# Row scatters of a routed-experts kernel: spaced over attention's units, the last 24 at the start of the last stage

## The reference

```python
logits = xt @ router_w.T + routing_bias
probs = jax.nn.sigmoid(logits)
topk_p, topk_idx = jax.lax.top_k(probs, TOP_K)          # TOP_K = 2
topk_p = topk_p / jnp.sum(topk_p, axis=-1, keepdims=True)
...
h = jax.nn.silu(g) * u                                  # per expert
y = jnp.einsum('tei,ehi->teh', h, wd)
routed = jnp.einsum('te,teh->th', w, y)
return (shared + routed).reshape(orig_shape)
```

## Time and profile before

| what | value |
|---|---|
| median of 3 runs | 1726.43 us (1722.62 to 1728.62) |
| the profiled execution | 1709.23 us |
| its span | 1707.4 us |
| mean granted TensorE clock | 0.945 |
| attention, first to last instruction | 595.45 to 1159.44 us |
| last stage begins | 1165.07 us |

### The profile page before, as it was taken

One profiled execution on the slowest core, in us unless ns is written; L12 is line 12 of the kernel. 1 busy time (PEld: TensorE's weight loads), 2 busy tenths in 40 slices (PEclk: granted clock), 3 DMA queues, 4 the chain that ended last, 5 costly groups with the idle time before them and its releaser, 6 DMA issues. The chain is left out here.

```text
span 1707.4 us, 28845 instructions
## 1 busy us (share of the span) xinstructions
PE 1508.1 (88%) x10278; PEld 1160.2 (68%) x10278; DVE 1105.0 (65%) x2324; ACT 903.8 (53%) x1123; POOL 448.2 (26%) x439
## 2 busy tenths in 40 slices
PE   5899999698999888999988987765899999999996
PEld 4788888577878652444343433344689999999985
DVE  5577776678878845546735645243457778777757
ACT  2566546255555435565554554532246777777741
POOL 1122232130101122211423333145202333333324
PEclk8999999889999979999988999976799999999998
DMA  7000000210000002100000000014116888888844
GB/s 260 1 1 0 0 0 0 75 40 1 0 0 0 7 19 89 64 1 1 21 7 27 1 26 27 10 48 166 46 37 189 230 237 234 231 235 236 227 116 148
DMA packets 65068, 130.47 MB, mean 76 GB/s; under 512 B 8377, under 2 KB 38882, under 8 KB 64482
## 3 DMA queue, kind: packets, MB, share of 16 engines
q1 hardware_dynamic: 49922, 108.14, 20.6%
q0 software_dynamic: 15072, 21.37, 5.7%
HBM read 97.50 MB, written 32.00 MB: 76 GB/s over the span
## 5 line engine op out<-in xcount | busy, mean ns | idle before, releaser
L1745 ACT ACTIVATE at_wide<-at_sc_ps 128x2048 f32<-128x2048 f32 x128 | 240.6, 1880 | 176.6 <-PE at_sc_ps L1590 169.7
L1590 PE MATMUL at_sc_ps<-at_qT,at_kT 32*128 32x512 f32 x1024 | 152.4, 665 | 59.7 <-ACT at_wide L1745 55.1
L2168 POOL DMA_INDIRECT sums<-e_y,e_row_ids x78 | 121.7, 1560 | 313.8 <-ACT e_y L2323 301.9
L52 PE MATMUL e_gate_ps<-e_h_parts,e_w 128*128 128x256 f32 (+1 forms) x1128 | 179.3, 307 | 10.4 <-DVE e_w L2374 3.9
L52 PE MATMUL e_up_ps<-e_h_parts,e_w 128*128 128x256 f32 (+1 forms) x1128 | 175.8, 303 | 0.0
L2374 DVE TENSOR_TENSOR e_w<-e_raw,e_w 128x1024 fp32r<-128x1024 f32 x123 | 147.3, 1223 | 42.0 <-ACT e_w L2276 42.0
L52 PEld LDWEIGHTS e_gate_ps<-e_h_parts,e_w 128*128 128x128 f32 x1128 | 156.8, 195 | 18.8 <-issue 7.0
L52 PEld LDWEIGHTS e_up_ps<-e_h_parts,e_w 128*128 128x128 f32 x1128 | 156.1, 193 | 8.3
L1604 PE MATMUL at_o_ps<-at_wide,at_v_ones 128*32 128x512 f32 x1024 | 142.4, 629 | 1.1 <-ACT at_wide L1745 1.1
L2239 PE MATMUL e_down_ps<-e_w,e_hidden 128*128 128x256 f32 x936 | 127.9, 286 | 1.1 <-DVE e_hidden L2423 1.1
L2276 ACT ACTIVATE e_w<-e_raw 128x1024 fp32r<-128x1024 f32 x123 | 125.3, 1048 | 4.0 <-DMA e_raw<-in_experts 4.0
(11 more groups left out here) (348 smaller groups left out, 2718.2 us busy)
## 6 DMA issues: line engine op xcount, KB each, us to landing
e_raw<-in_experts SPq DMA_DIRECT2D x123, 512.0 KB
e_rows_in<-slots SPq DMA_DIRECT2D x39, 272.0 KB
sums<-shared SPq DMA_DIRECT2D x17, 256.0 KB
x<-in_L_attn_x SPq DMA_DIRECT2D x8, 512.0 KB, 9.5
gate<-gates SPq DMA_DIRECT2D x4, 1024.0 KB, 4.7
out<-x SPq DMA_DIRECT2D x7, 512.0 KB, 3.1
e_sums<-sums SPq DMA_DIRECT2D x4, 512.0 KB, 4.6
shared<-sums SPq DMA_DIRECT2D x4, 512.0 KB, 5.2
```

The lines of the kernel that those rows point to most:

```text
L52: last = pe.matmul(out, left(i), right(j), start=n == 0, stop=n == len(steps) - 1)
L1590: last = nc.tensor.matmul(sc_ps[:, m, :], kT[strip, par, quad % 2, quad // 2, k * P:(k + 1) * P], qT[strip, par, quad // 2, :], start=True ...
L1745: nc.scalar.activation(wide[:, u % 2, :], sc_ps[:].rearrange("p n s -> p (n s)"), ACT.Sigmoid, scale=float(HD) ** -0.5).then_inc(sig_done, 1)
L2168: pool.indirect_dma_start(c.sums_dram[:, :], bass.IndirectOffsetOnAxis(ap=row_ids[:, j % 2, t:t + 1], axis=0), y[:, j % 2, t, :], None, co ...
```

## The change

In attention, `scatter` is split into `tag` (waits and tag copies) and single scatters. In iteration b of 3 and more the tags of batch b - 3 and its first scatter come right behind `place_values`; the others follow one by one between GpSimd's other pieces, each waiting until 3, 5, 7, ... 15 sigmoids of the iteration are done. The scatters of batches 5, 6 and 7 leave attention and the place behind it: GpSimd issues all 24 as the last stage begins. (A pace by `hidden_split` is written for those from number `UNPACED` = 24 on, which are none.) The rows of batch 7 are made and kept in the last stage, behind its first step, which is written out ahead of the loop for this. The padding is one plain DMA per expert on SP's queue, with its address read from `pads`.

```diff
-                    if b >= 3:
-                        ds.scatter(pool, b - 3)
...
+                def scatter(b, n, unit=None):
+
+                    if b >= 3:
+                        if unit is not None:
+                            pool.wait_ge(sig_done, UNITS * b + unit)
+                        ds.scatter(pool, b - 3, n)
...
                     if coming:
                         place_values(b + 1, 1 - par, early)
+                    if b >= 3:
+                        ds.tag(pool, b - 3)
+                    scatter(b, 0)
+                    if coming:
                         times_cos(b + 1, 0)
+                    scatter(b, 1, 3)
+                    if coming:
                         times_cos(b + 1, 1)
+                    scatter(b, 2, 5)
                     if past:
                         bias_x(b - 1)
+                    scatter(b, 3, 7)
+                    if past:
                         norm.invert(pool, b - 1)
+                    scatter(b, 4, 9)
                     if coming:
                         times_cos(b + 1, 2)
+                    scatter(b, 5, 11)
+                    if coming:
                         times_cos(b + 1, 3)
+                    scatter(b, 6, 13)
+                    scatter(b, 7, 15)
...
                 bias_x(B - 1)
-                ds.scatter(pool, B - 3)
                 norm.invert(pool, B - 1)
-                ds.scatter(pool, B - 2)
...
-                pe.wait_ge(ds.rows_kept, 2 * (B - 1))
-                ds.make_rows(pe, B - 1, 0, sc_ps[:, 0, :])
-                ds.make_rows(pe, B - 1, 1, sc_ps[:, 1, :])
...
-                ds.keep_rows(act, B - 1, 0, sc_ps[:, 0, :])
-                ds.keep_rows(act, B - 1, 1, sc_ps[:, 1, :])
...
+                for e in range(E):
+                    at = sp.value_load(pads[0:1, e:e + 1], min_val=0, max_val=E * REGION - TS)
+                    sp.dma_start(c.slots_dram[bass.ds(at, TS)].rearrange("(p t) r -> p t r", p=P), ds.empty
+                                 ).then_inc(ds.padded, 16)
...
-                ds.scatter(pool, B - 1)
-                pool.wait_ge(listed, 1)
-                for e in range(E):
-                    for t in range(TT):
-                        pool.indirect_dma_start(c.slots_dram, bass.IndirectOffsetOnAxis(ap=pads[:, e, t:t + 1], axis=0),
-                                                ds.empty[:, t, :], None).then_inc(ds.padded, 16)
+                LATE = 3
+                for k in range(LATE * 2 * NT):
+                    b = B - LATE + k // (2 * NT)
+                    if k % (2 * NT) == 0:
+                        ds.tag(pool, b)
+                    if k >= UNPACED:
+                        pool.wait_ge(hidden_split, k - UNPACED + 1)
+                    ds.scatter(pool, b, k % (2 * NT))
...
-                with pe.Fori(0, BEFORE) as n:
+                step(0, 0, 1)
+                pe.wait_ge(ds.placed, B)
+                pe.wait_ge(listed, 1)
+                for half in range(2):
+                    ds.make_rows(pe, B - 1, half, tp_ps[:, half, :])
+                with pe.Fori(1, BEFORE) as n:
                     step(n, n * IC, 1)
+                pe.wait_ge(ds.rows_kept, 2 * B)
...
-                with act.Fori(0, BEFORE - 1) as n:
+                step(0, 0, 1)
+                for half in range(2):
+                    ds.keep_rows(act, B - 1, half, tp_ps[:, half, :])
+                with act.Fori(1, BEFORE - 1) as n:
                     step(n, n * IC, n + 1)
...
-                    nc.vector.scalar_tensor_tensor(out=pads[:], in0=ends[:].unsqueeze(2).broadcast_to([P, E, TT]), scalar=BIG,
-                                                   in1=pad_at[:].unsqueeze(1).broadcast_to([P, E, TT]), op0=ALU.add, op1=ALU.add)
+                    nc.vector.tensor_scalar(pads[:], ends[:], BIG, None, ALU.add)
```

More of the change, by code:

```diff
@@ L1346, in keep_rows, with tag @@
                                   ACT.Copy).then_inc(self.rows_kept, 1)
-    def scatter(self, pool, b):
+    def tag(self, pool, b):
         c = self.c
@@ L1358, in scatter @@
         pool.wait_ge(self.placed, b + 1)
[L1359 to L1363, removed]
+    def scatter(self, pool, b, n):
+        t, which = n // 2, n % 2
+        at = NT * b + t
+        pool.indirect_dma_start(self.c.slots_dram, bass.IndirectOffsetOnAxis(ap=self.slots[:, which, at:at + 1], axis=0),
+                                self.rows[:, b % 2, t, :], None).then_inc(self.scattered[b % 2], 16)
 class AttentionTables:
@@ L2036, in silu_experts_part @@
         tile_expert, tile_base = sb("tile_expert", [P, TILES], I32), sb("tile_base", [P, TILES], I32)
-        pads, pad_i, pad_at = sb("pads", [P, E, TT], I32), sb("pad_i", [P, TT], I32), sb("pad_at", [P, TT])
+        pads = sb("pads", [P, E], I32)
         of_tile = sb("of_tile", [P, TILES, E])
@@ L2064, in silu_experts_part @@
              "taken y_done added x_done stored").split())
+        UNPACED = 24
         ORDER = [0, 1, 2, 3, 7, 4, 5, 6]
@@ L2109, in _ @@
                     load_weights(1, q, here)
+                for e in range(E):
+                    at = sp.value_load(pads[0:1, e:e + 1], min_val=0, max_val=E * REGION - TS)
+                    sp.dma_start(c.slots_dram[bass.ds(at, TS)].rearrange("(p t) r -> p t r", p=P), ds.empty
+                                 ).then_inc(ds.padded, 16)
                 for u in range(2):
                     sp.wait_ge(ds.scattered[u], ds.PER_BATCH * B // 2)
-                sp.wait_ge(ds.padded, 16 * E * TT)
+                sp.wait_ge(ds.padded, 16 * E)
                 load_rows(0)
@@ L2147, in _ @@
             def _(pool):
-                pool.iota(pad_i[:], pattern=[[P, TT]], base=0, channel_multiplier=1)
                 pool.iota(counts_i[:, 0:RUNGS], pattern=[[TS, RUNGS]], base=0, channel_multiplier=0)
@@ L2152, in _ @@
                 pool.wait_ge(tables_set, 1)
-                nc.gpsimd.tensor_copy(pad_at[:], pad_i[:])
                 nc.gpsimd.tensor_copy(ladder[:], counts_i[:, 0:RUNGS])
```

## The result

| | before | changed |
|---|---|---|
| median | 1724.75 us (1722.62 to 1728.62, 4 runs) | 1659.23 us (1658.23 to 1659.91, 4 runs) |
| ratio | | 0.9617, 95% interval 0.9597 to 0.9637 |
| profiled execution, its span | 1709.23, 1707.4 | 1658.23, 1656.5 |
| mean granted clock | 0.945 | 0.961 |

A forecast was written before the change was run, and what follows sets the result against it. TensorE, busy for 88% of the span, was taken to be held up by GpSimd's scatter bursts and the low clock behind them. -27 - 7.8 + 2.5 = -32.3 us gave 1676.9 profiled and a median of 1694, range 1678 to 1722.

The forecast's parts named there:

- The rival on which the stall was not the scatters': Late `modulate` belongs to its place in the code or to traffic that stays; 1721 us, chance 0.09.
- Iterations 3 to 6, 24.7 us: Attention: spacing the scatters removes 4.29 us from iteration 3 and 6.79 us from each of the next three.
- the signs: Attention, if right: no "remote" waits, `modulate` within 0.6 us, iterations 3 to 6 near 61 us, granted clock 1.00 throughout.
- The end of attention, 10.4 us with iteration 7: Behind the loop: moving late scatters and batch 7's rows out saves 7.8 us; iteration 7 was put at 2.6.
- The offset: Whole kernel: profiled execution lies 17.2 us under the runs' median, so 1676.9 us profiled becomes a median of 1694.1.
- The last stage, +2.5 us: Last stage: bursts cost the same as before; transposes 1.2 us and later weights 1.3 us add 2.5; bounds -8 and +15.
- 14.0 and 6.8, together 20.8 against 20.7: nothing: Last stage: its two new bursts, at 0.66 us per us, cost 20.8 us against 20.7 for the old one.
- its lower bound of -8: Last stage: the first burst hides in the 9.6 us before the first matmul, which wait anyway.
- In every burst the first four or five scatters delayed nobody: All bursts of the kernel before: the argument against the rival in which every single scatter stalls somebody.
- the slower rival: Attention: each spaced scatter delays a sigmoid by itself, 1.4 us each, 56 us in all; 1750 us, chance 0.13.
- The last stage takes it back: Last stage: the burst meets the start-up, so the upper bound of +15 us holds; 1707 us, chance 0.12.
- The choice of the issuer: Skill statement set against the change: issuer choice saves only issue time, so spacing or SP pads should not free another engine.

The follow-up runs named there:

- the added scatters: Changed kernel with six more indirect scatters in each of iterations 3 to 6, to a tensor nobody reads: 1687.56 us with whole rows, 1684.76 us with rows of 16 floats.
- the second profile: The kernel before, unchanged, profiled and timed again: 1724.53 us, ratio 1.0004; its profiled execution has a span of 1727.3 us.
- The kernel with paced scatters: Changed kernel with UNPACED 8 instead of 24, so the scatters of batches 6 and 7 wait for one `hidden_split` each: 1654.61 us, ratio 0.9592.
- pairs: Changed kernel with an iteration's eight scatters in four pairs, behind the start and the sigmoids of units 5, 9 and 13: 1658.44 us, ratio 0.9682.
- the kernel with pauses: Kernel before with GpSimd clearing a tile behind each scatter but the last in the attention loop's five bursts, nothing moved: 1682.49 us, ratio 0.9844.
- the long row of 24: Changed kernel with the padding back on GpSimd, 16 indirect DMAs behind the eight scatters of batch 7: 1676.9 us, ratio 0.9719.
- the row behind `bias_x`: Changed kernel with all eight scatters of an iteration in one burst behind `bias_x`, some 15 us earlier than before's burst: 1674.88 us, ratio 0.9802.
- the fours: Changed kernel with an iteration's eight scatters in two groups of four, the second behind the 14th sigmoid, beside `modulate`: 1673.23 us, ratio 0.9695.
- five undisturbed variants: Variants differing from the changed kernel in next to nothing but harmless DMAs or the pace of scatters: 1654.6 to 1658.9 us.

## Why the prediction was half right

**That the bursts stall the other engines, and not a place in the code:** right. The rival on which the stall was not the scatters' is refuted by the run with only the spacing and by the added scatters.

**Iterations 3 to 6, 24.7 us:** right for the profile it was read from (24.1). Against the second profile, which lay 4.5 us above its median where the first lay 15 to 17 below, it was 37.2: `modulate` waits longer there, and the low clock lasts longer behind it. The clean iteration was sized from iteration 2 at full clock (61.16 for 61.30 measured). The clock was not 1.00 throughout, as the signs had it: over the first 8 us it was 1.00 in iterations 5 and 7 and 0.79 in 4 and 6.

**The end of attention, 10.4 us with iteration 7:** 12.4 by the same profile, within the bounds given, and 19.6 against the second. The gap to the last stage was priced too low: it shrank from 5.66 us to 1.03 (1127.68 to 1128.71), so 4.6 us for the 2 that were taken.

Two steps failed, by 16.2 and 17.0 us. The sum for the profiled execution was 1676.9 and came to 1658.23, and the median lay 1.0 above that and not 17.2.

**The offset.** The prediction added the 17.2 us by which the first profile lay under the median, as if they belonged to every kernel alike. They belonged to the stall and the low clock behind it: the second profile of the unchanged kernel has 13.1 us more in iterations 3 to 6 and 7.1 between them and the last stage, together its 19.9 us within 0.3. Iteration 2, without scatters, took 57.7 us in both. What is taken away with the stall takes its spread along.

**The last stage, +2.5 us.** Up to the turning of tile 0's rows it saved 13.3 (1278.68 - 1165.10 = 113.6 before, 1228.94 - 1128.71 = 100.2 after). The failed term is "14.0 and 6.8, together 20.8 against 20.7: nothing", with its rate of 0.66 us of stall for each us of burst. By the same reckoning (steps 0 and 1 less twice 16.66, without the transposes) the two late rows cost 7.1: 23.78 - 0.87 + 17.52 - 33.32. The kernel with paced scatters, which shows no stall, has 2.4 of that as well, so that is step 0's own start; the scatters cost 18.3 before and 4.7 after, which are the 4.6 us that pacing gains. The price is not a rate per us of burst: a stall begins only some us into an unbroken row and goes on about as long as it does. Before, 24 DMAs stood in one row of 31.3 us. Changed, the first eight (1130.28 to 1142.46) begin 7.4 us ahead of the first matmul (1137.66) and delay nobody: the paced kernel issues them in the same way and shows no stall. The next eight follow the first tags at once, the last eight only at 1162.98, and each of the two ends in a stall. The prediction had this as its lower bound of -8 ("the first burst hides") and not in its sum. Taking the 16 pads out of the row, priced at nothing as a mere exchange of one burst for another, was worth 18.5 us alone. The rest of the term held: the transposes cost 0.87 (1.2 predicted), and the first matmul came 0.65 us earlier in the stage, not 1.3 later.

**"In every burst the first four or five scatters delayed nobody":** so in the traces of before, but wrong as a rule. Behind the third of four `modulate` was held, 1.6 us; pairs held nobody. That a scatter by itself costs nothing was right, and it decided the sign: the slower rival, each single scatter delaying somebody, is refuted by the sigmoid gaps of iterations 3 to 6: from the fourth gap on they are those of iteration 2 to 0.04 us, but for three that are 0.3 longer.

**The last stage takes it back:** it didn't. First matmul 8.95 us into the stage and steps 0 and 1 41.3 us together, against 15 and 70.

**The choice of the issuer.** Six plain DMAs cost nothing on SyncE's queue or on GpSimd's (1658.5 and 1657.7 us), while moving the 16 indirect pads to SyncE as plain ones saved 18.5 us, and others' time, not issue time. The Trainium skill ("DMA: Bandwidth & Descriptors", section "Issuing engines are not separate DMA queues") has the choice of issuer save issue time alone. The plain DMAs agree with that. The 18.5 us don't speak against it, since the padding changed its kind along with its issuer, and it is the kind that the added DMAs show to matter; no run has an indirect DMA of another issuer. So the prediction set the statement against the wrong thing: it says nothing of the kind of DMA, and the gain came from there.

**What stays open.** Which resource the rows of indirect DMAs take from the others. It isn't bandwidth (short rows) or the issuing queue (plain DMAs). All the waits that were looked at, `modulate`, the gating and the sigmoid, wait for TensorE. In attention its instructions are not late by their records: in iteration 3 of before it runs the transposes at 849.81, the next scores at 850.78 and the next products at 851.85, spaced as in the kernel with pauses (849.55, 850.51, 851.59), and yet `modulate` starts at 853.37 and the sigmoid of those scores at 856.24. So there it is the news of TensorE's work that comes late (the ends of matmuls are modelled in the profile, so this is short of shown). In the long row of 24 its instructions are late as well: from 1177.57 to 1197 it runs one to five matmuls at a time, with up to 0.8 us between them in which it waits for nothing that the profile shows. That a backlog builds up at 1.27 us and not at 1.79 fits all runs, but is argued: the profile shows no such backlog. Why a sigmoid 4.9 us into the row behind `bias_x` is on time and `modulate` 3.5 us into the fours is not, is open too, and so is why the stall of the same kernel is longer in some executions and before slower in some series: the chip isn't the whole reason, since the series with before at 1724.1 and those at 1712.5 and 1709.4 have the same one on record.

## What to carry to other kernels

Look at the "remote" waits in a profile and see whether they lie in a row of GpSimd's indirect DMAs; if so, put a pause of half a microsecond or other work between them, or a plain DMA in their place, before anything is rescheduled. Take the profiled execution's distance from the median apart before carrying it over: if it sits in the stall that the change removes, it goes with it. Price a stall by how long the row is behind its first few, not by a rate, and add what the low clock costs behind it, which can be more than the stall.

## What the runs showed of the hardware

- Indirect DMAs of 128 rows 1.27 us apart, four and more in a row, held ScalarE and VectorE up, for 1 to 20 us by the length of the row; 1.79 us apart, or in pairs, they held up nobody, and nor did the first eight of the last stage in the paced kernel. With six of the eight at 64 bytes a row instead of 1,088 nearly as much was lost (26.3 us and 29.1).
- Behind a stall at the iteration's end TensorE's scores took 2.09 us instead of 1.14, at a granted clock of 0.50, and the start of the next iteration was up to 5.0 us longer. Over its first 8 us the clock was 0.50 in the second profile of before, 0.71 to 0.85 in the first, and 0.79 or 1.00 in the changed kernel.
- Six plain DMAs of 139 KB in each of four iterations, at the same moment, cost nothing that shows on GpSimd's queue (1657.7 us) and on SyncE's (1658.5), against 1659.2 without them.
- The same kernel's median was 1724 to 1728 us in some series and 1709 to 1712 in others. The medians of the changed kernel and its five undisturbed variants, over four series, stayed within 1654.6 to 1659.2. Two profiles of before, 19.9 us apart, differ where the rows of attention stall and just behind; that this is the spread of the medians too is likely, not shown.
